# Sixty-four bytes ahead of the rounded weights in SBUF

## The chip, the cores and the metric

The kernel runs on one core of one Trainium2 chip. The metric is the device time of one execution in microseconds. The kernel before takes 237.88 us (median of three runs, 237.66 to 238.07).

## What is computed

Inputs: `x` [64, 64, 512], `cond` [64, 256], all float32. Cut to what matters:

```python
q_emb = relu(cond @ W3 + b3)                              # [64, 512]
x1    = (64 * x + x.sum(axis=1, keepdims=True)) * q_emb[:, None, :]
y     = relu(x1 @ W2 + b2)                                # [4096, 512] @ [512, 512]
base  = y @ W_base + b_base                               # 512 -> 512
h     = y @ [W_router, A_s, A_r]                          # 6 + 16 + 96 columns
gates = softmax(router logits), the two largest kept
out   = x + base + (A_s part) @ B_s + (A_r part * gates) @ B_r
```

## The kernel before, in words

The 4096 tokens go in eight groups of 512. Every factor of a large product is kept as two float32r tiles: the rounded value (`_hi`) and the rest that rounding dropped (`_lo`). A product is three matmuls: hi times hi, hi times lo, lo times hi. Every one of these matmuls reads a 128x128 weight block into the array (the stationary operand) and then streams 512 columns of float32 past it (the moving operand); 512 float32 are 2048 bytes of a partition.

TensorE (PE) goes through each group in a written order, in `step` of its block:

- `m1`: four output blocks, 12 matmuls each. A 128-column block of `W2_hi` or `W2_lo` is stationary, a chunk of `x1_hi` or `x1_lo` moves.
- `h`: 12 matmuls. A chunk of `Wd_hi` or `Wd_lo` is stationary, a chunk of `y_hi` or `y_lo` moves.
- `m2`: four token blocks, 12 matmuls each. A 128-token block of `y_hi` or `y_lo` is stationary, a chunk of `Wb_hi` or `Wb_lo` moves.
- `up`: 12 matmuls for the group before. A block of `hw_hi` or `hw_lo` is stationary, `Wu_hi` or `Wu_lo` moves.

So a group is 120 matmuls, 60 with a weight tile as the stationary operand and 60 with a weight tile as the moving operand. In eight groups that is 960, and one more (`expand`, `pick` stationary and `w_quads` moving) in the last group. `product` (line 743) issues nearly all of them; `m1_first` (line 770) those of the first group's `m1`.

VectorE (DVE) turns x, sums over tokens, and makes the rests of x1, y and hw. ScalarE (ACT) makes the rounded values, in the head also those of the weights (lines 368, 387, 391, 430). GpSimd (POOL) makes the rests of the weights in the head (line 310) and scales x1. SP issues the loads and stores. Semaphores tie the engines together; nothing in the order of the instructions depends on where a tile lies.

Tiles lie in SBUF in the order in which `sb(...)` allocates them, one behind the other in each partition. The first, `edge`, is 1920 bytes that nothing reads, so `x_nat0` begins at byte 18432, which is 9 times 2048. All tiles from there to `gatesT` are multiples of 2048 bytes, so each begins at a multiple of 2048: `x1_hi` 88064, `y_hi` 120832, `hw_hi` 141312, `W2_hi` 165888, `Wb_hi` 182272, `Wd_hi` 198656, `Wu_hi` 202752, `w_quads` 206848. Inside a tile, a chunk of 512 float32 begins at a multiple of 2048 too, and a 128-column block of it 0, 512, 1024 or 1536 bytes behind one.

Of the kernel before, what the change touches and what calls it, by code (L numbers as in the profile page):

```python
# [22 lines left out]
def adaln_ffn(nc, x, cond, W3, b3, W2, b2, W_base, b_base, A_s, B_s, A_r, B_r, W_router, b_router, out):  # L23
# [6 lines left out]
    P = 128  # L30
# [26 lines left out]
    with ctx:  # L57
        def sb(name, shape, dt=F32):
            return ctx.enter_context(nc.sbuf_tensor(name, shape, dt))
# [24 lines left out]
        Wb_f = sb("Wb_f", [P, KC, D])  # L84
        Wd_f = sb("Wd_f", [P, KC, P])
        Wu_f = sb("Wu_f", [P, D])
        W2_hi = sb("W2_hi", [P, KC, D], F32R)
        W2_lo = sb("W2_lo", [P, KC, D], F32R)
        Wb_hi = sb("Wb_hi", [P, KC, D], F32R)
# [2 lines left out]
        Wd_lo = sb("Wd_lo", [P, KC, P], F32R)  # L92
        Wu_hi = sb("Wu_hi", [P, D], F32R)
        Wu_lo = sb("Wu_lo", [P, D], F32R)
        w_quads = sb("w_quads", [P, TG], F32R)
        gatesT = sb("gatesT", [P, TG])

# [816 lines left out]
```

## Time and profile before

| what | value |
|---|---|
| median of three runs | 237.88 us |
| the profiled execution's own time | 238.09 us |
| its span, first to last instruction | 236.2 us |
| granted TensorE clock, mean | 0.999 |
| PE busy, share of the span | 98% |
| PEld (weight loads) busy | 80% |
| DVE, ACT, POOL busy | 71%, 37%, 21% |

The profile names engines PE (matmul), PEld (weight load, which overlaps PE), DVE, ACT, POOL and SP. L743 is line 743. Matmuls are pipelined, so the records of two in a row overlap; the time from one start to the next, called pitch below, is what one costs. The ends of matmuls are modelled, their starts are not. Buffer numbers are left out of the names: `x_hi` is `x1_hi`, `W_hi` is `W2_hi`, `m_ps` is any of the PSUM banks of `m1` and `m2`.

### The profile page before, as it was taken

How to read it: one execution, taken by the hardware profiler on the slowest of the kernel's cores; microseconds unless marked ns; L12 is line 12 of the kernel's file. 1: busy time of each engine (PE TensorE's matmuls, PEld its weight loads, DVE VectorE, ACT ScalarE, POOL GpSimd, SP SyncE). 2: the span in 40 equal slices, each digit the busy share in tenths (PEclk: the TensorE clock that was granted, in tenths of full speed). 3: DMA queues.
4: the chain of work that ended last, by engine and by line, in shares of the span. 5: the costliest groups of instructions: out<-in, count | busy, mean ns of one | idle time of the engine just before them, and what ended most of it. 6: DMA issues, size and time to landing. Idle time of an engine off the chain costs nothing.

```text
span 236.2 us, 3092 instructions
## 1 busy us (share of the span) xinstructions
PE 230.7 (98%) x1008; PEld 188.2 (80%) x1008; DVE 166.7 (71%) x309; ACT 86.3 (37%) x171; POOL 49.0 (21%) x57
## 2 busy tenths in 40 slices
PE   7999899999999999999999999999999999999994
PEld 2988587878888888888888888888888888888883
DVE  0694999698979978398747969299665976055344
ACT  2266851535136240353206340263305351152330
POOL 6179342022123211022012030122110130000000
PEclk9999999999999999999999999999999999999999
DMA  7999902618043541706245451709120270104004
GB/s 198 317 218 224 277 17 40 172 56 300 8 117 89 195 163 29 182 29 221 112 87 121 175 183 18 179 14 298 57 33 0 111 244 12 22 0 178 3 0 178
DMA packets 33009, 28.80 MB, mean 122 GB/s; under 512 B 6325, under 2 KB 23413, under 8 KB 32998
## 3 DMA queue, kind: packets, MB, share of 16 engines
q1 hardware_dynamic: 31194, 28.50, 42.9%
q10 hardware_dynamic: 1804, 0.17, 0.6%
q8 instruction: 6, 0.10, 0.2%
q14 instruction: 5, 0.04, 0.1%
HBM read 18.89 MB, written 8.39 MB: 115 GB/s over the span
## 4 chain that ended last, share of the span: by engine, by line
PE 87%; SPq 6%; DVE 2%; DMA 2%; issue 0%; DVEq 0%
PE m_ps L743 78%; PE hT L743 9%; SPq L206 3%; DMA x_quart<-in_x_dram 2%; DVE out_nat L621 1%; SPq L228 1%; SPq L222 1%; SPq L225 1%; SPq L232 1%; DVE xT L467 0%; DVE vsum L472 0%; DVE x_sum L479 0%; SPq L229 0%; DVE y_lo L493 0%; SPq L231 0%
## 5 line engine op out<-in xcount | busy, mean ns | idle before, releaser
L304 POOL TENSOR_TENSOR x_full<-x_sum,qT 128x512 f32<-128x512 f32 x28 | 32.4, 1157 | 136.8 <-DVE x_sum L479 136.8
L348 ACT ACTIVATE y_hi<-m_ps,b_sb 128x512 fp32r<-128x512 f32 x32 | 22.0, 687 | 82.3 <-PE m_ps L743 80.3
L743 PE MATMUL m_ps<-Wb_hi,y_lo 128*128 128x512 f32 x128 | 49.9, 390 | 0.0
L743 PE MATMUL m_ps<-Wb_lo,y_hi 128*128 128x512 f32 x128 | 49.9, 390 | 0.0
L743 PE MATMUL m_ps<-Wb_hi,y_hi 128*128 128x512 f32 x128 | 49.9, 390 | 0.0
L743 PE MATMUL m_ps<-x_hi,W_hi 128*128 128x512 f32 x112 | 43.9, 392 | 0.0
L743 PE MATMUL m_ps<-x_lo,W_hi 128*128 128x512 f32 x112 | 43.7, 390 | 0.0
L743 PE MATMUL m_ps<-x_hi,W_lo 128*128 128x512 f32 x112 | 43.6, 390 | 0.0
L493 DVE TENSOR_TENSOR y_lo<-m_ps,y_hi 128x512 fp32r<-128x512 f32 x32 | 21.7, 679 | 30.2 <-ACT m_ps L350 30.2
L467 DVE STREAM_TRANSPOSE xT<-x_quart 128x512 f32<-128x512 f32 x28 | 30.4, 1087 | 3.1 <-DMA x_quart<-in_x_dram 3.1
L743 PEld LDWEIGHTS m_ps<-Wb_lo,y_hi 128*128 128x128 f32 x128 | 24.0, 188 | 5.0
L743 PEld LDWEIGHTS m_ps<-Wb_hi,y_lo 128*128 128x128 f32 x128 | 24.0, 188 | 4.9
L743 PEld LDWEIGHTS m_ps<-Wb_hi,y_hi 128*128 128x128 f32 x128 | 24.0, 188 | 4.9
L743 PEld LDWEIGHTS m_ps<-x_hi,W_hi 128*128 128x128 f32 x112 | 21.0, 188 | 5.0 <-DVE x_lo L487 0.7
L743 PEld LDWEIGHTS m_ps<-x_hi,W_lo 128*128 128x128 f32 x112 | 21.0, 188 | 4.3
L743 PEld LDWEIGHTS m_ps<-x_lo,W_hi 128*128 128x128 f32 x112 | 21.0, 188 | 4.3
L342 ACT ACTIVATE x_hi<-x_full 128x512 fp32r<-128x512 f32 x28 | 17.5, 628 | 17.7 <-POOL x_full L304 17.7
L621 DVE TENSOR_TENSOR out_nat<-m_ps,x_nat 128x512 f32<-128x512 f32 x32 | 20.5, 680 | 2.1 <-PE m_ps L743 2.1
L487 DVE TENSOR_TENSOR x_lo<-x_full,x_hi 128x512 fp32r<-128x512 f32 x28 | 19.3, 707 | 2.5 <-ACT x_hi L342 2.3
L350 ACT ACTIVATE m_ps<-m_ps,b_sb 128x512 f32<-128x512 f32 x32 | 21.0, 655 | 0.0
L479 DVE SCALAR_TENSOR_TENSOR x_sum<-xT,vsum 128x512 f32<-128x512 f32 x28 | 19.4, 692 | 2.1
L472 DVE TENSOR_REDUCE vsum<-xT 128x8 f32<-128x512 f32 x28 | 19.1, 683 | 0.4
(97 smaller groups left out, 256.4 us busy)
## 6 DMA issues: line engine op xcount, KB each, us to landing
out_dram<-out_nat SPq DMA_DIRECT2D x32, 256.0 KB, 2.2
x_quart<-in_x_dram SPq DMA_DIRECT2D x28, 256.0 KB, 4.7
x_nat<-in_x_dram SPq DMA_DIRECT2D x7, 1024.0 KB, 6.0
gatesT<-wT SPq DMA_DIRECT2D x28, 48.0 KB
x_nat<-in_x_dram SPq DMA_DIRECT2D x4, 256.0 KB, 3.6
W_f<-in_L_cond_W_dram SPq DMA_DIRECT2D x4, 256.0 KB, 7.5
Wb_f<-in_L_ffn_W_base_dram SPq DMA_DIRECT2D x1, 1024.0 KB, 9.8
W_sb<-in_L_cond_W_dram SPq DMA_DIRECT2D x1, 512.0 KB, 6.1
```

Of the source, the lines that this page charges most:

```text
L206: eng.dma_start(Wd_f[:, k, RO:P].rearrange("p (e r) -> p e r", r=R), A_r[:, k * P:(k + 1) * P, :].rearrange("e p r -> p e r")).then_inc(Wd ...
L304: nc.gpsimd.tensor_tensor(per_batch(x1_full[:, c, :]), per_batch(x1_sum[:, c, :]), qT[:, c, bass.ds(BG * g, BG)].unsqueeze(2).to_broadcast ...
L342: nc.scalar.activation(x1_hi[par][:, c, :], x1_full[:, c, :], ACT.Copy).then_inc(x1_hi_ready, 1)
L348: nc.scalar.activation(y_hi[:, m, :], m1_ps[m][:, :], ACT.Relu, bias=b2_sb[:, m:m + 1]).then_inc(y_hi_ready, 1)
L350: nc.scalar.activation(m1_ps[m][:, :], m1_ps[m][:, :], ACT.Relu, bias=b2_sb[:, m:m + 1]).then_inc(y_full_ready, 1)
L467: nc.vector.transpose(xT[c % 2][:, :], x_quart[par][:, :, :].rearrange("p b (i c) -> p c b i", c=KC)[:, c]).then_inc(xT_ready, 1)
L472: nc.vector.tensor_reduce(vsum[c % 2][:, :], per_batch(xT[c % 2][:, :]), AX.X, ALU.add).then_inc(vsum_ready, 1)
L479: nc.vector.scalar_tensor_tensor(out=per_batch(x1_sum[:, c, :]), in0=per_batch(xT[c % 2][:, :]), scalar=float(N), in1=vsum[c % 2][:, :].un ...
L487: nc.vector.tensor_tensor(x1_lo[par][:, c, :], x1_full[:, c, :], x1_hi[par][:, c, :].bitcast(F32), ALU.subtract).then_inc(x1_lo_ready, 1)
L493: nc.vector.tensor_tensor(y_lo[:, m, :], m1_ps[m][:, :], y_hi[:, m, :].bitcast(F32), ALU.subtract).then_inc(y_lo_ready, 1)
L621: nc.vector.tensor_tensor(out_nat[par][:, t, :], m2_ps[t][:, :], x_nat[par][:, t, :], ALU.add).then_inc(out_ready, 1)
L743: mm = nc.tensor.matmul(psum, lhsT, rhs, start=start and i == 0, stop=stop and i == len(terms) - 1)
```

## The change

Two tiles are allocated that no instruction touches: 64 bytes ahead of the weights' rounded tiles, and 192 bytes behind the last of them. The eight tiles `W2_hi`, `W2_lo`, `Wb_hi`, `Wb_lo`, `Wd_hi`, `Wd_lo`, `Wu_hi` and `Wu_lo` then begin 64 bytes behind a multiple of 2048 (`W2_hi` at 165952, `Wb_hi` at 182336, `Wd_hi` at 198720, `Wu_hi` at 202816). The tiles before them stay where they are, x1, y and hw among them. All tiles behind them (`w_quads`, `gatesT`, `idle`, `pick`, the small ones) lie 256 bytes further on. No instruction is added, removed or moved on any engine; the streams differ in nothing but line numbers and addresses.

```diff
         Wd_f = sb("Wd_f", [P, KC, P])
         Wu_f = sb("Wu_f", [P, D])
+        quarter_line = sb("quarter_line", [P, 16])
         W2_hi = sb("W2_hi", [P, KC, D], F32R)
         W2_lo = sb("W2_lo", [P, KC, D], F32R)
...
         Wu_hi = sb("Wu_hi", [P, D], F32R)
         Wu_lo = sb("Wu_lo", [P, D], F32R)
+        line_rest = sb("line_rest", [P, 48])
         w_quads = sb("w_quads", [P, TG], F32R)
```

## Rows read from the trace of the kernel before

**Rows 1.** The page: span, then busy us (share of span), instructions.
```profile
span 236.2 us, 3092 instructions
PE 230.7 (98%) x1008; PEld 188.2 (80%) x1008; DVE 166.7 (71%) x309; ACT 86.3 (37%) x171; POOL 49.0 (21%) x57
```
**Rows 2.** The chain that ended last: its shares, then pieces (start us, us, what).
```profile
PE 87%; SPq 6%; DVE 2%; DMA 2%; issue 0%; DVEq 0%
...
30.17 23.08 PE m_ps L743 x99
53.25 2.04 PE hT L743 x9
55.29 1.36 PE m_ps L743 x6
56.65 0.68 PE hT L743 x3
57.33 23.12 PE m_ps L743 x102
80.45 2.04 PE hT L743 x9
```
**Rows 3.** Timeline of PE from 99.7 us (start us, us, what).
```profile
99.78 0.39 PE L743 MATMUL m_ps<-x_hi,W_lo 128*128 128x512 f32 x1
...
101.82 0.39 PE L743 MATMUL m_ps<-x_hi,W_lo 128*128 128x512 f32 x1
102.05 0.39 PE L743 MATMUL m_ps<-Wu_hi,hw_hi 128*128 128x512 f32 x1
...
103.86 0.39 PE L743 MATMUL m_ps<-Wu_hi,hw_lo 128*128 128x512 f32 x1
```
**Rows 4.** Timeline of PE from 8 us.
```profile
8.26 1.03 PE L720 MATMUL m_ps<-idle 128*128 128x512 bf16 x4
9.12 3.73 PE L763 MATMUL m_ps<-condT,W_sb 128*128 128x64 f32 x16
```
**Rows 5.** Timeline of PE from 39.7 us.
```profile
39.76 0.39 PE L743 MATMUL m_ps<-x_lo,W_hi 128*128 128x512 f32 x1
39.98 0.39 PE L743 MATMUL m_ps<-x_hi,W_lo 128*128 128x512 f32 x1
40.33 0.50 PE L743 MATMUL m_ps<-x_hi,W_hi 128*128 128x512 f32 x1
40.67 0.39 PE L743 MATMUL m_ps<-x_lo,W_hi 128*128 128x512 f32 x1
40.90 0.40 PE L743 MATMUL m_ps<-x_hi,W_lo 128*128 128x512 f32 x1
41.17 0.50 PE L743 MATMUL m_ps<-x_hi,W_hi 128*128 128x512 f32 x1
41.52 0.40 PE L743 MATMUL m_ps<-x_lo,W_hi 128*128 128x512 f32 x1
41.76 0.40 PE L743 MATMUL m_ps<-x_hi,W_lo 128*128 128x512 f32 x1
41.99 0.40 PE L743 MATMUL m_ps<-x_hi,W_hi 128*128 128x512 f32 x1
42.23 0.40 PE L743 MATMUL m_ps<-x_lo,W_hi 128*128 128x512 f32 x1
42.46 0.39 PE L743 MATMUL m_ps<-x_hi,W_lo 128*128 128x512 f32 x1
```
**Rows 6.** Timeline of PEld in the same stretch (in brackets idle before, releaser).
```profile
39.76 0.19 PEld L743 LDWEIGHTS m_ps<-x_hi,W_lo 128*128 128x128 f32 x1
40.33 0.19 PEld L743 LDWEIGHTS m_ps<-x_hi,W_hi 128*128 128x128 f32 x1 [0.38 <-DVE x_lo L487]
40.44 0.19 PEld L743 LDWEIGHTS m_ps<-x_lo,W_hi 128*128 128x128 f32 x1
```
**Rows 7.** Groups by line and shape: count, busy us, mean ns, idle before.
```profile
L310 POOL TENSOR_TENSOR W_lo<-W_f,W_hi 128x512 fp32r<-128x512 f32 x4 | 5.1, 1286 | 7.7 <-ACT W_hi L368 7.7
...
L368 ACT ACTIVATE W_hi<-W_f 128x512 fp32r<-128x512 f32 x4 | 2.4, 621 | 0.0
L391 ACT ACTIVATE Wb_hi<-Wb_f 128x512 fp32r<-128x512 f32 x4 | 2.2, 623 | 0.0
...
L733 PE MATMUL m_ps<-ident,x_nat 128*128 128x128 f32 x12 | 2.7, 354 | 0.0
```

## The prediction, made before the changed kernel ran

> **What bounds the kernel.** I read the page's busy shares first, then the chain of waits, then the timeline of PE in a quiet stretch. PE is busy for 230.7 of 236.2 us [rows 1], and the chain that ended last is PE for 87% of the span; the rest is the head, in which loads and SP's queue are late, and the last additions [rows 2]. From 57.33 us to 80.45 us the chain is one piece of 102 matmuls with no wait in it: 23.12 us / 102 = 226.7 ns each. The piece before it, and the short ones of hT between (2.04 us / 9 = 226.7 ns), go at the same pace [rows 2]. So the time is a count of matmuls times a pitch, plus a head and a tail, and a change of place in SBUF is worth what it does to the pitch. At 2.4 GHz (the granted clock is 0.999) 512 columns are 213.3 ns; 226.7 ns are 544 cycles, 32 more than columns.
>
> The reader is to see that this number is the same wherever I look. With W2 stationary and x1 moving, nine pitches lie between 99.78 and 101.82 us: 2.04 / 9 = 226.7 ns. With hw stationary and Wu moving, eight lie between 102.05 and 103.86 us: 1.81 / 8 = 226 ns, within the rounding of two starts [rows 3]. The piece of 102 holds blocks of W2, Wu and Wb whose stationary operands begin 0, 512, 1024 and 1536 bytes behind a multiple of 2048, and it has one pace [rows 2]. An offset of 512 bytes between the two operands therefore costs nothing. No row has an offset of 64.
>
> **The change, part by part.**
>
> *The streams.* Nothing is added, removed or moved; no wait, transfer or count differs. All that can change is the duration of an instruction that reads or writes a shifted tile.
>
> *Matmuls, 480 with a weight tile stationary.* Their weight loads now read 512 bytes from 64 bytes further on. A load hides beside the matmul before it: loads start with that matmul (39.76 beside 39.76 us), and two loads in a row after a wait lie 40.44 - 40.33 = 0.11 us apart, so a load needs about half of a pitch [rows 5, 6]. It could become 100 ns longer before a matmul waited for it. By itself the shift costs these nothing; what is left is that load and stream disturb each other by their relative place.
>
> *Matmuls, 480 with a weight tile moving.* Their 2048 bytes now begin 64 bytes behind a multiple of 2048 and cross one such multiple. The 32 surplus cycles over 2048 bytes are one per 64 bytes, or one per 16 columns. If they belong to the stream itself, they come again at every 64 bytes whatever multiple of 64 it begins at, and the shift is by just that: nothing again. Is the surplus of the stream itself? Two matmuls run with no load beside them: the one at 39.98 us (the next load is at 40.33) and the one at 40.90 us (the next matmul, whose load starts with it, is at 41.17). Their records last 0.39 and 0.40 us, as long as records with a load beside them [rows 5, 6]. Ends are modelled, so this is a hint and no proof, but it says that no contest with the weight load makes the 32 cycles.
>
> *Bounds of the pitch.* Since no row has the offset, both ends come from the nearest rows. From below: the four bfloat16 matmuls of 512 columns at 8.26 us, which read half as many bytes, take (9.12 - 8.26) / 4 = 215 ns; the length of their joint record says the same: less the 0.16 us by which a float32 record of 0.39 outlasts its pitch of 0.227, (1.03 - 0.16) / 4 = 217 ns, and I use 216 [rows 3, 4]. That is 10.7 ns less than now. From above: after a wait the same float32 matmuls go slower for about ten of them. From 41.52 to 42.46 us four pitches take 0.94 us, 235 ns each, 8 ns more than in the quiet stretch, with the same operands at the same places [rows 5]. So the pitch does move with something other than the operands' names, namely with the moment at which load and stream start against each other, and this is the one sign in the trace that places could matter. Per half of the matmuls (480), -10.7 ns are -5.1 us and +8 ns are +3.8 us; for a single clock cycle, 480 x 0.417 ns = 0.2 us. I take zero, the row of the quiet stretch: it is by far the nearest in operands, count and order, and it holds four offsets without a difference.
>
> A rule of the Trainium skill (TensorE: Matmul & The Clock Gate, Back-to-back issue gap) gives a warm matmul its columns over 2.4 GHz plus 2.5 ns, with no term for the type: 215.8 ns for 512. The bfloat16 rows agree at 216, the float32 rows do not at 226.7; if that surplus were a matter of places alone and the shift cured it, an estimate by this page would be 237.9 - 960 x 10.9 ns = 227.4 us, which is the first rival at its full size. The same page (Part 2, What happens when you issue a matmul) states that the stream and the weight load have independent read ports and take no bandwidth from each other; by that both rivals below would fall, while the 235 ns after a wait are something that it has no place for.
>
> *The head.* Eight writes of ACT and POOL to W2 and its rests, eight to Wb, and four to Wd and Wu go to shifted tiles, 621 to 623 ns each on ACT and 1286 on POOL [rows 7]; each tile is still one run of 2048 bytes. If a crossed multiple cost a hundredth of one, that is 13 ns on POOL, and eight in a row on the path are 0.1 us; I take zero. The 16 transposes read `ident` 256 bytes further on, 354 ns a record [rows 7]; as they wait for loads, a hundredth of them is under 0.02 us. `expand` is one matmul, `gatesT` off the path.
>
> *Sum.* 238.09 us of the profiled execution (span 236.2, 1.9 around it) plus 0 = 238.09; that execution lies 0.2 us above the median of the runs, so the forecast is 237.9 us.
>
> **Rivals.** What a measurement can tell from no change is about 0.2%, 0.5 us, or about 1.2 cycles over one half of the matmuls.
>
> *The shift takes part of the surplus away.* Now all three, stream, load and results, begin at a multiple of 2048, so if it is the same place that makes two readers meet, load and stream meet at the start of every matmul; 64 bytes apart they would not. For it speaks the bfloat16 pitch [rows 4] and that the pitch varies after a wait [rows 5]. Against it speak that 512 bytes change nothing [rows 2, 3] and that a matmul without a load beside it is as long [rows 5, 6]. As the two halves have the offset with opposite sign (in one the load is ahead, in the other the stream), one half is likelier than both: 237.9 - 5.1 = 232.8 us; both: 227.6 us.
>
> *The shift makes the stream slower.* The place is the 480 matmuls of `m2` and `up`, whose stream now ends in the next 2048 bytes, or the lock between load and stream, which in the quiet stretch settles at 226.7 ns and might settle where it stands after a wait, at up to 235. For it speaks that the slower pace exists with the same operands [rows 5]; against it that the chain's pieces always come back to 226.7 [rows 2]. One half: 237.9 + 3.8 = 241.7, or 241 if it settles at 233; both halves: 245.5. Nothing hides it, since PE never waits in the pieces of 102; it decides from the first cycle on, at 0.2 us a cycle and half.
>
> *The change does not do what it says.* The allocator could have padded the tiles away; the addresses in the built program show that it did not, so this has no chance of its own.
>
> **How the numbers follow.** No change: 0.52, within 237.4 to 238.4. Faster in one half 0.13, in both 0.07; by a cycle or two 0.02: 0.22 together. Slower in one half 0.14, in both 0.07, by some cycles 0.05: 0.26 together. The range reaches from the faster half to the slower half, 232.8 to 241.7, and leaves out both full cases, 0.14. The likeliest case's own range is 237.4 to 238.4.
>
> **What would show it.** The timeline of PE in a quiet stretch: 226.7 ns from start to start with W2 stationary and with Wb or Wu moving, and a chain with pieces of 102 matmuls in 23.12 us. A piece of another length says that the pitch moved; whether starts in `m1` or those in `m2` are apart by another step says which operand did it. A load that is longer than 0.19 us beside an unchanged pitch would show a cost that stayed hidden. I am wrong if the span differs by more than 0.5 us, and wrong in the reason if it differs in the head.

## The result, and the profile after

The changed kernel takes 242.49 us (median of four runs, 242.23 to 242.69), the kernel before 237.87. The ratio is 1.0197, 95% interval 1.018 to 1.0214: slower by 4.6 us, and outside the predicted range of 232.8 to 241.7. The two profiled executions differ by less, 242.23 - 238.09 = 4.1 us: that of after is the fastest of its four.

The page of after, answering to [rows 1] (same columns):

```profile
span 240.3 us, 3092 instructions
PE 235.2 (98%) x1008; PEld 188.2 (78%) x1008; DVE 167.9 (70%) x309; ACT 86.4 (36%) x171; POOL 49.1 (20%) x57
```

The span grew by 4.1 us, PE's busy time by 4.5, that of its loads by nothing. The chain of after (start us, us, what), answering to [rows 2]:

```profile
29.93 23.07 PE m_ps L745 x99
53.01 2.10 PE hT L745 x9
...
57.21 23.59 PE m_ps L745 x102
80.80 2.10 PE hT L745 x9
...
84.99 23.76 PE m_ps L745 x102
```

The first piece of 102 begins at 57.21 us, before at 57.33, and the piece of 99 ahead of it takes 23.07 us, before 23.08: the head, the first group and the start of the second cost nothing in this trace. From there each piece is longer: 23.59 and 23.76 us against 23.12, and the nine of hT go at 233 ns. A busy-time window of each kernel from that point to the last matmul's start gives the whole loss in one subtraction. Each row has the bounds, the length in us, the busy time (count) of PE, PEld, DVE, ACT and POOL, then the granted clock, DMA's share and GB/s; of before first, then of after:

```profile
57.33:232.60 175.27, 175.27 (x775) 145.24 (x774) 123.66 (x241) 59.43 (x118) 25.36 (x22) 1.00 0.34 100
```

```profile
57.21:236.60 179.39, 179.39 (x775) 145.34 (x774) 124.10 (x241) 59.52 (x118) 25.37 (x22) 1.00 0.33 97
```

The same 775 matmuls without a wait, at the same clock, in 179.39 instead of 175.27 us: 4.12 us, 5.3 ns each. The timeline of PE in after shows the step (start us, us, what); nine pitches answer to those of [rows 3]:

```profile
98.12 0.39 PE L745 MATMUL m_ps<-x_hi,W_hi 128*128 128x512 f32 x1
98.35 0.40 PE L745 MATMUL m_ps<-x_lo,W_hi 128*128 128x512 f32 x1
98.59 0.39 PE L745 MATMUL m_ps<-x_hi,W_lo 128*128 128x512 f32 x1
98.82 0.40 PE L745 MATMUL m_ps<-x_hi,W_hi 128*128 128x512 f32 x1
...
100.22 0.40 PE L745 MATMUL m_ps<-x_hi,W_hi 128*128 128x512 f32 x1
...
116.23 0.39 PE L745 MATMUL m_ps<-Wb_hi,y_hi 128*128 128x512 f32 x1
...
116.92 0.39 PE L745 MATMUL m_ps<-Wb_hi,y_hi 128*128 128x512 f32 x1
```

With W2 stationary 98.12 to 100.22 us are 2.10 / 9 = 233.3 ns, in turn 231 and 236. With Wb moving, three pitches take 116.92 - 116.23 = 0.69 us, 229 to 230 ns. Over all pitches without a wait the half with a stationary weight averages 233.4 ns and the half with a moving one 230.8, before 227.0 and 226.9. The 230.8 is a mixture: `m2` settles at 229 ns in five of the eight groups and at 233.3 in three, with the same addresses. The piece of 23.59 us is of the first kind, that of 23.76 of the second: 42 matmuls of `m2` at 4 ns more are the 0.17 us between them.

### The profile page after: what moved, and what is told of

Its sections match the earlier page's. It is cut to its first block, busy times and chain, and to the rows that moved or that the text cites. A ratio compares the mean times of both kernels' runs of the same rounds, so it can differ in the third digit from the quotient of the medians.

```text
span 240.3 us, 3092 instructions
## 1 busy us (share of the span) xinstructions
PE 235.2 (98%) x1008; PEld 188.2 (78%) x1008; DVE 167.9 (70%) x309; ACT 86.4 (36%) x171; POOL 49.1 (20%) x57
## 4 chain that ended last, share of the span: by engine, by line
PE 87%; SPq 6%; DVE 3%; DMA 2%; issue 0%; DVEq 0%
PE m_ps L745 78%; PE hT L745 9%; SPq L208 3%; DMA x_quart<-in_x_dram 2%; DVE out_nat L623 1%; SPq L224 1%; SPq L230 1%; SPq L227 1%; DVE x_sum L481 1%; DVE xT L469 0%; SPq L234 0%; DVE vsum L474 0%; DVE y_lo L495 0%; SPq L233 0%; SPq L231 0%
## 5 line engine op out<-in xcount | busy, mean ns | idle before, releaser
L745 PE MATMUL m_ps<-Wb_hi,y_lo 128*128 128x512 f32 x128 | 50.5, 395 | 0.0
L745 PE MATMUL m_ps<-x_hi,W_hi 128*128 128x512 f32 x112 | 44.4, 396 | 0.0
L745 PE MATMUL m_ps<-x_lo,W_hi 128*128 128x512 f32 x112 | 44.3, 395 | 0.0
L745 PE MATMUL m_ps<-x_hi,W_lo 128*128 128x512 f32 x112 | 44.3, 395 | 0.0
L481 DVE SCALAR_TENSOR_TENSOR x_sum<-xT,vsum 128x512 f32<-128x512 f32 x28 | 20.0, 716 | 2.1
```

The lines of the kernel that those rows point to most:

```text
L481: nc.vector.scalar_tensor_tensor(out=per_batch(x1_sum[:, c, :]), in0=per_batch(xT[c % 2][:, :]), scalar=float(N), in1=vsum[c % 2][:, :].un ...
L745: mm = nc.tensor.matmul(psum, lhsT, rhs, start=start and i == 0, stop=stop and i == len(terms) - 1)
```

## The experiments

**A table of pitches, and where both operands are shifted.** Behind the last matmul of the kernel before, blocks of 40 float32r matmuls, with `W2_hi` stationary from byte a of its tile and `x1_hi0` moving from byte b:

```diff
+def pairs(a, b, cols, width, n):
...    # W_flat, x_flat: W2_hi and x1_hi0 with one index for all columns
+    for _ in range(n):
+        nc.tensor.matmul(m1_ps[0][0:cols, 0:width], W_flat[:, a // 4:a // 4 + cols],
+                         x_flat[:, b // 4:b // 4 + width], start=True, stop=True)
```

> The kernel before with a table of pitches behind its last matmul: 16 blocks of 40 float32r matmuls (128 stationary columns, 512 moving), the stationary operand begins a bytes and the moving operand b bytes behind a multiple of 2048, (a, b) = (0,0) (64,0) (0,64) (64,64) (128,0) (0,128) (192,0) (0,192) (256,0) (0,256) (32,0) (16,0) (4,0) (512,0) (64,128) (0,0); then 40 with 32 stationary columns and 40 with 256 moving columns, both at (0,0). One bfloat16 matmul stands between blocks. Nothing else runs beside it. Its time as a whole says nothing. Theory A, the distance a - b decides: (0,0), (64,64) and (512,0) settle at 226.7 ns, (64,0) at 233.3 as W2 in the changed kernel, (0,64) at 229 as Wb there, (64,128) like (0,64). Theory B, each operand's own place decides, whatever the other's: (64,64) is at least as slow as (64,0), 233 ns or more, and (64,128) too. Theory C, the place matters only beside the other engines' traffic: all blocks at 226.7. If the 32 surplus cycles of a matmul belong to the stream, the 32-column block stays at 226.7 and the 256-column block takes 113.3; if they come from the weight load beside it, the 32-column block takes about 217 (8 cycles left of 32) and the 256-column block 120.

The timeline's bfloat16 matmuls, between which the first four blocks lie, and last the block with 256 moving columns:

```profile
232.11 0.39 PE L895 MATMUL m_ps<-idle 128*128 128x512 bf16 x1
...
241.45 0.39 PE L895 MATMUL m_ps<-idle 128*128 128x512 bf16 x1
...
251.02 0.39 PE L895 MATMUL m_ps<-idle 128*128 128x512 bf16 x1
...
260.42 0.39 PE L895 MATMUL m_ps<-idle 128*128 128x512 bf16 x1
...
269.76 0.39 PE L895 MATMUL m_ps<-idle 128*128 128x512 bf16 x1
...
392.45 5.13 PE L891 MATMUL m_ps<-x_hi,W_hi 128*128 128x256 f32 x40
```

Forty matmuls at (0,0), (64,0), (0,64) and (64,64) take 9.34, 9.57, 9.40 and 9.34 us: shifting both operands is as good as shifting none. From 241.45 us on no instruction of DVE, ACT or POOL runs beside them. Mean pitch of the last 20 matmuls of each block, in ns, from their starts:

```
(a,b)  (0,0)  (64,64)  (256,0)  (0,256)  (512,0)   226.7
       (64,0) (0,192)                              233.3
       (0,64) (192,0) (64,128)                     228.8 to 229.1
       (128,0) 232.4   (0,128) 233.3   (32,0) 233.4   (4,0) 232.3   (16,0) 226.7
       32 stationary columns 231.7     256 moving columns 120.0
```

Theory A holds for steps of 64 bytes, B and C fall: not an operand's own place but the distance between the two counts, with its sign, modulo 256 bytes, and it does so with no other engine running. At 128 bytes, where both signs are one distance, the two blocks still differ by 1 ns. The two last blocks do not fit one guess together: 256 columns take 120.0 ns, 288 cycles, so the surplus is 32 cycles again and not in proportion to the columns, while 32 stationary columns went slower, not faster.

**All tiles at 64.** `edge` is `[P, 496]` instead of `[P, 480]`.

> The first tile is 64 bytes longer, so that all tiles of the kernel, weights and x1, y, hw alike, begin 64 bytes behind a multiple of 2048. Theory A (the distance between the two operands of a matmul decides): 237.9 us, 226.7 ns in both kinds of matmul. Theory B (an operand that is off the multiple is slow by itself): at least 242.5, and up to 247 if the two add up.

238.91 us, ratio 1.005 (1.0033 to 1.0066). The pitches are back (226.9 ns in both halves) but 1.1 us stay. In the two kept traces, whose spans differ by 0.8 us, most of it is in the head, since the first piece of 102 begins at 57.97 us, before at 57.33: VectorE's first transpose of the next group waits for the x_quart load until 22.84 us, before until 22.14. Timeline of DVE, of this kernel and then of before:

```profile
22.84 1.09 DVE L467 STREAM_TRANSPOSE xT<-x_quart 128x512 f32<-128x512 f32 x1 [3.78 <-DMA x_quart<-in_x_dram]
```

```profile
22.14 1.11 DVE L467 STREAM_TRANSPOSE xT<-x_quart 128x512 f32<-128x512 f32 x1 [3.13 <-DMA x_quart<-in_x_dram]
```

In the eleven other kept traces, whose x_quart stayed in its place, this transpose begins at 21.05 to 22.14 us, so one trace at 22.84 does not show that the address made the load late.

**Only the matmuls' operands at 64.** The unrounded weights are allocated ahead of the 64 bytes, x1, y, hw and the rounded weights behind them, and 1984 bytes follow (the edit in short).

```diff
+W2_f, Wb_f, Wd_f, Wu_f        # moved up to here
+quarter_line = sb("quarter_line", [P, 16])
 x1_hi = ...
...
 Wu_lo = ...
+line_rest = sb("line_rest", [P, 496])
```

> All operands of the large matmuls (x1, y, hw and the rounded weights) lie 64 bytes behind a multiple of 2048, while everything that a load or store touches, the unrounded weights among it, stays at a multiple or where it was. Theory A (distance decides): 237.9 us, and the 1.1 us of the kernel with all tiles at 64 came from its loads. If it is the operands off a multiple that cost the 1.1 us (through the writes of ACT, DVE and POOL): 238.9 again.

237.92 us, ratio 0.9995 (0.9981 to 1.001), and its chain has the pieces of before:

```profile
57.17 23.12 PE m_ps L745 x102
```

So reading and writing these operands off a multiple of 2048 costs nothing that shows, and the 1.1 us of the kernel with all tiles at 64 belong to what this one leaves in place: its loads' targets, or another tile outside the products. Which of them was not tried.

**One half at a time.** In the first kernel only W2 and Wd lie at 64, in the second only Wb and Wu; the other pair and all behind it are at multiples of 2048 (the edit in short).

```diff
+quarter_line = sb("quarter_line", [P, 16])
 W2_hi, W2_lo, Wd_hi, Wd_lo    # second kernel: Wb_hi, Wb_lo, Wu_hi, Wu_lo
+line_rest = sb("line_rest", [P, 496])
 Wb_hi, Wb_lo, Wu_hi, Wu_lo    # second kernel: W2_hi, W2_lo, Wd_hi, Wd_lo
```

> Only W2 and Wd, the stationary weights, lie 64 bytes behind a multiple of 2048; Wb and Wu, which move, are back at a multiple, as is all behind them. If each half of the matmuls pays for its own distance: 480 matmuls at 233.3 instead of 226.7 ns, 237.9 + 3.2 = 241.1 us, with Wb moving at 226.7. If the stationary operand's place were nothing and only the moving one's crossing of a multiple cost: 237.9. If one slow half spoils the pace of the other: 242.5.

240.62 us, ratio 1.0123 (1.0106 to 1.014): near the 241.1 of each half paying for itself; the stationary half at 233.5 ns, the moving one at 227.5. Its chain:

```profile
56.83 23.48 PE m_ps L745 x102
```

> Only Wb and Wu, the moving weights, lie 64 bytes behind a multiple of 2048; W2 and Wd are back at a multiple, as is all behind them. If each half pays for its own distance: 480 matmuls at 229 to 231 ns instead of 226.7, 237.9 + 1.1 to 2.1 = 239.0 to 240.0 us, with W2 stationary at 226.7. If only the crossing by the moving operand cost: 242.5. If the cost were all on the stationary side: 237.9.

241.22 us, ratio 1.0149 (1.0132 to 1.0166), more than any branch that lets each half pay for itself. The moving half averages 232.2 ns: in one of its eight groups `m2` settles at 229, in seven at 233.3, at one and the same distance. The stationary half, at distance 0, averages 228.7, since it settles anew after each change of distance: from the third group on the 12 matmuls of `m1` behind `up` average 230.8 ns, and the 9 of `h` that follow are back at 226.7. Its chain:

```profile
56.66 23.53 PE m_ps L745 x102
80.19 2.04 PE hT L745 x9
```

Alone the halves lose 2.8 and 3.4 us, together 4.6 in the changed kernel, where `m2` fell into the slower pace in three groups and not in seven.

**256 bytes.** `quarter_line` is `[P, 64]`, the rest fills up to 2048.

> The eight rounded weight tiles lie 256 bytes behind a multiple of 2048 instead of 64, x1, y and hw at a multiple, all behind the weights at a multiple again. Theory A with a period of 256 bytes, as the table has it: 237.9 us with 226.7 ns in both kinds of matmul. Theory B (off a multiple of 2048 is slow, at whatever distance): 242.5.

237.97 us, ratio 1.0011 (0.999 to 1.0032): no difference, and its chain is again

```profile
57.06 23.12 PE m_ps L745 x102
```

**Every matmul at one distance.** W2 and Wd at 64 with Wb and Wu at 192 makes the stationary operand begin 64 bytes behind the moving one everywhere; the other way round makes it -64.

```diff
+pad_a = sb("pad_a", [P, 16])
 W2_hi, W2_lo, Wd_hi, Wd_lo    # -64: Wb_hi, Wb_lo, Wu_hi, Wu_lo
+pad_b = sb("pad_b", [P, 32])
 Wb_hi, Wb_lo, Wu_hi, Wu_lo    # -64: W2_hi, W2_lo, Wd_hi, Wd_lo
+pad_c = sb("pad_c", [P, 464])
```

> The stationary weights W2 and Wd lie 64 bytes behind a multiple of 2048, the moving ones Wb and Wu 192 behind one, x1, y and hw and all else at multiples. So the stationary operand of every large matmul begins 64 bytes behind the moving one, modulo 256. Theory A (the signed distance modulo 256 decides): all 961 matmuls at 233.3 ns instead of 226.7, 237.9 + 6.3 = 244.2 us, with no difference between the two halves. Rival, each kind of tile has its price (a stationary weight off a multiple of 256 costs 6.6 ns, a moving one some 4): as the changed kernel, 242.5.

> The mirror image: Wb and Wu 64 bytes behind a multiple of 2048, W2 and Wd 192 behind one, so that the stationary operand of every large matmul begins 64 bytes ahead of the moving one, modulo 256. Theory A: all matmuls in the pace of the blocks with that distance, 229 ns, 237.9 + 2.2 = 240.1 us; as the kernel with only Wb and Wu moved showed both 229 and 233.3 ns at this distance, up to 244.2 if it falls into the slower one each time. Rival, each kind of tile has its price: 242.5, with W2 stationary at 233.

243.26 us, ratio 1.0225 (1.0206 to 1.0243), and 240.32 us, ratio 1.0099 (1.008 to 1.0118). The chains, of +64 and then of -64:

```profile
57.42 23.78 PE m_ps L746 x102
81.20 2.10 PE hT L746 x9
```

```profile
57.30 23.39 PE m_ps L746 x102
80.69 2.06 PE hT L746 x9
```

At +64 both halves settle at 233.3 ns in every group, at -64 both at 228.9: Wb, which went at 229 or 233 in after, now goes at 233 at 192 bytes, and W2, which went at 233, goes at 229. The rival by kinds of tile, 242.5 us for both, falls. The -64 kernel came within 0.2 us of its 240.1. The +64 kernel is 0.9 us better than its 244.2, which charged all 961 matmuls: its first piece of 102 begins at 57.42 us, before at 57.33, so the matmuls ahead of it paid next to nothing, and the 775 from there on at 6.6 ns are 5.1 us.

**Other distances, and whether a distance fixes the pace.**

> A second table behind the last matmul of the kernel before, made as the first: blocks of 40 matmuls with the stationary operand a bytes behind a multiple of 2048 and the moving one at it, a = 16, 32, 48, 80, 96, 112, 144, 160, 176, 208, 224, 240, 8, 248, 1024, 0; then, both at a multiple, 40 with 64 stationary columns, 40 with 384 and 40 with 448 moving columns. Its time as a whole says nothing. Theory A as the first table left it (the distance modulo 256 decides, 0 and 16 settle at 226.7 ns, 32, 64, 128 and -64 slower): 1024 and 0 at 226.7, 16 and 32 as before (226.7 and 233.3). If the surplus of 32 cycles is the floor of a float32r matmul whatever the distance, no block goes below 226.7 and the blocks with 384 and 448 moving columns take 384 + 32 and 448 + 32 cycles, 173.3 and 200 ns. If distance 0 is itself one of the disturbed places, some block settles below, at 216 ns as bfloat16 does, and the kernel has up to 10 us to gain.

```
a (b = 0)   0, 1024, 144: 226.7   240: 228.4   176: 230.0   8: 230.7   80: 232.0
            16, 32, 48, 112, 208, 224, 248: 233.3   160: 233.5   96: 234.5
64 stationary columns 230.3   384 moving columns 173.4   448 moving columns 202.7
```

> A third table behind the last matmul of the kernel before: for 1, 2, 3 and 4 bfloat16 matmuls ahead of the block, blocks of 40 matmuls with the stationary operand 16, 64 and 192 bytes behind the moving one; then 60 matmuls whose stationary operand is in turn 0 and 64 bytes behind, and 60 in turn 0 and 192. Its time as a whole says nothing. If a distance alone fixes the pace, each distance settles at one number whatever stands ahead (64 at 233.3, 192 at 229). If a distance allows several rhythms and the start picks one, 16 and 192 settle at different numbers from block to block (16 gave 226.7 in the first table and 233.3 in the second). In the mixed blocks, if only the load that runs beside a stream counts, the two kinds of matmul in turn have two pitches, or both settle at 226.7 or above together if the rhythm carries over.

```
bfloat16 matmuls ahead     1       2       3       4
stationary 16 behind    233.4   233.3   233.4   226.7
           64 behind    233.4   233.3   233.3   233.4
          192 behind    228.8   228.8   228.8   229.1
0 and 64 in turn 230.0           0 and 192 in turn 230.0
```

No block of 512 columns goes below 226.7, so no distance tried gains anything over the kernel before. The block with 448 columns missed its 200 ns: 202.7 are 38 to 39 cycles more than columns, though both operands lie at multiples, and no run says why. Some distances have two paces: 16 (226.7 in the first table, 233.3 in the second, both here) and -64 (228.8 here, 229 or 233.3 in `m2`). At 16 it is what ran ahead of the block that picks one. The mixed blocks settle together in one repeating row of pitches, so whether it is the load beside a stream or the one ahead of it that counts stays open.

## Why the prediction was wrong

What bounds the kernel was right: a count of matmuls times a pitch, and all of the loss is in the pitch [rows 2]. That no instruction and no load's record changes, and that the head costs nothing, held too: PEld is busy for 188.2 us as before, and ACT's and POOL's writes to the shifted tiles of W2 go at 622 and 1290 ns against 621 and 1286 [rows 7].

```profile
L370 ACT ACTIVATE W_hi<-W_f 128x512 fp32r<-128x512 f32 x4 | 2.4, 622 | 0.0
L312 POOL TENSOR_TENSOR W_lo<-W_f,W_hi 128x512 fp32r<-128x512 f32 x4 | 5.1, 1290 | 7.6 <-ACT W_hi L370 7.6
```

The step that failed is "I take zero, the row of the quiet stretch", because "it holds four offsets without a difference". Those four, 0, 512, 1024 and 1536, are one and the same offset modulo 256, as the table shows; the rows spoke of a single point of the period and I read them as a flat line. In place of zero the two traces show 5.3 ns a matmul, 4.1 us in all, and the experiments that it goes by the distance between the two operands' addresses modulo 256.

A second step made zero look cheaper than it was. The 32 surplus cycles were shared out as one per 64 bytes of the stream, so that a shift by 64 had to be harmless. One per 64 bytes would be 16, 24 and 28 cycles at 256, 384 and 448 columns; those blocks take 32, 32 and 38 to 39 more than columns (120.0, 173.4 and 202.7 ns). The surplus is not in proportion to the bytes of the stream, and the argument from 64 bytes had no ground. The records without a load beside them, 0.39 and 0.40 us [rows 5, 6], were taken for a sign against a contest of load and stream. Their length could not bear that; the table, where the pitch goes by the distance between the load's and the stream's addresses, shows that the two do interact. What they share, so that 256 bytes are the period, no run shows.

The row that pointed the right way is [rows 5]: 235 ns after a wait with the same operands, though that it has the same cause is not shown. [rows 5] lie in the piece of 99, which goes at 23.08 / 99 = 233.1 ns with its waits and not, as the prediction says of the piece before that of 102, at the same pace. The slower rival named that pace, a lock that "might settle where it stands after a wait, at up to 235", and at distance 64 it settles at 233.3. It had 0.26, and its price for one half was 3.8 us; both halves were hit, the stationary one by 6.4 ns and the moving one by 3.9, which the range left out. The faster rival fell on its mechanism's sign: no distance tried is faster than 0. Two small sums were off without changing the forecast: 0.5 us over one half of the matmuls are 2.5 cycles and not 1.2, and a hundredth of 16 records of 354 ns is 0.06 us and not under 0.02.

Of the Trainium skill, the independent read ports (TensorE: Matmul & The Clock Gate, What happens when you issue a matmul) do not make load and stream independent here: 6.6 ns a matmul at distance +64. Its floor of columns plus 2.5 ns (Back-to-back issue gap), 215.8 for 512, is met by no float32r block at any distance tried; the lowest measured is columns plus 32 cycles.

## What to carry to other kernels

Where float32r matmuls follow each other without a wait, read the pitch from start to start, and compare it with columns plus 32 cycles (met here at 256, 384 and 512 columns, not at 448); a pitch of 229 to 235 ns for 512 columns can be a matter of addresses alone. Let stationary and moving operands begin at the same place modulo 256 bytes: here that is worth up to 2.2% against a distance of 64, and multiples of 256 are as good as multiples of 2048. When rows at several offsets agree, ask whether they are different offsets at all before calling the effect flat.

## What was not expected of the hardware

The pace is not a smooth function of the distance: 128, 144 and 160 bytes give 232.4, 226.7 and 233.5 ns. A few settled rows of pitches, at 226.7, 228.9 and 233.3 ns, come again and again, with others between them, and at distance 16 the same block settled at 226.7 or 233.3 by what ran ahead of it. Narrowing the stationary operand to 32 columns slowed the matmul from 226.7 to 231.7 ns, in the one block that tried it.
